# Transposing the attention probabilities with DMA engines in 16-bit halves, in one stage of an eight-layer kernel on Trainium2

## What is computed

```python
q = (hidden_states @ Wq).reshape(B, Sq, H, D)          # H = 16 heads, D = 128
k = (encoder_hidden_states @ Wk).reshape(B, Skv, H, D)
v = (encoder_hidden_states @ Wv).reshape(B, Skv, H, D)
q = rmsnorm(q, gq); k = rmsnorm(k, gk)
scores = jnp.einsum('bqhd,bkhd->bhqk', q, k) * scale
attn = jax.nn.softmax(scores, axis=-1)
out = jnp.einsum('bhqk,bkhd->bqhd', attn, v)
return out.reshape(B, Sq, H * D) @ Wo
...
x = x + jnp.tanh(g_xattn[1]) * _L1_xattn_ref(_layernorm(x, axis=-1), ctx_1024, ...)
```

## Time and profile before

| | |
|---|---|
| median of 3 runs | 1055.78 us (1053.52 to 1056.75) |
| the profiled execution | 1059.89 us |
| its span, first to last instruction | 1058.6 us |
| PE busy | 936.7 us (88%) |
| DVE busy | 725.1 us (68%) |
| ACT busy | 520.7 us (49%) |
| POOL busy | 302.5 us (29%) |
| first attention's loop | about 247 to 554 us of the span |
| PE busy, 285 to 325 us | 40.00 of 40 us, granted clock 1.00 |
| DVE busy, 285 to 325 us | 27.72 of 40 us |
| PE busy, 480 to 520 us | 39.67 of 40 us, granted clock 1.00 |
| DVE busy, 480 to 520 us | 29.76 of 40 us |
| POOL busy, 285 to 325 us | 7.43 of 40 us |

### The profile page before, as it was taken

How to read it: one execution, slowest core, us unless ns; L and a number is a source line. 1 busy time by engine, 2 the same in 40 slices (tenths; PEclk the granted TensorE clock), 3 DMA queues, 4 the chain that set the end, 5 groups by cost and what they waited for, 6 DMA issues and landing times.

```text
span 1058.6 us, 14861 instructions
## 1 busy us (share of the span) xinstructions
PE 936.7 (88%) x4790; PEld 669.3 (63%) x4790; DVE 725.1 (68%) x1877; ACT 520.7 (49%) x1346; POOL 302.5 (29%) x284
## 2 busy tenths in 40 slices
PE   7878789999999999999999989877589988979667
PEld 3323334567999998888977767754355655545455
DVE  5899894245777677678676445576978965576764
ACT  4665672135666666566653434354346552123331
POOL 3767692121111112155101324234232200010210
PEclk8878899999999999999999999999899999989789
DMA  9500001001111164113103446312100003211201
GB/s 363 228 0 0 1 0 50 1 30 45 35 41 46 45 236 153 31 62 94 46 1 119 147 133 191 128 65 60 51 1 1 2 1 141 78 46 31 87 1 41
DMA packets 28500, 75.00 MB, mean 71 GB/s; under 512 B 4092, under 2 KB 5382, under 8 KB 27656
## 3 DMA queue, kind: packets, MB, share of 16 engines
q1 hardware_dynamic: 24344, 63.81, 17.6%
q0 software_dynamic: 3072, 8.39, 2.5%
q10 hardware_dynamic: 1008, 1.86, 0.6%
HBM read 52.03 MB, written 22.02 MB: 70 GB/s over the span
## 4 chain that ended last, share of the span: by engine, by line
PE 62%; DVE 15%; ACT 3%; issue 3%; DMA 1%; SPq 1%; POOL 1%; another core or an unknown queue 0%; DVEq 0%; POOLq 0%; ACTq 0%
PE psum L2195 5%; PE psum L1071 5%; PE psum L1796 5%; PE psum L1277 4%; PE psum L1288 4%; PE psum L927 4%; PE psum L1257 4%; PE psum L1268 2%; PE psum L938 2%; PE psum L1810 2%; PE psum L1095 2%; PE psum L2214 2%; PE psum L2816 2%; PE psum L2458 2%; DVE arena L2492 2%
## 5 line engine op out<-in xcount | busy, mean ns | idle before, releaser
L1167 POOL TENSOR_TENSOR arena<-arena,mhalf 128x8 f32<-128x8 f32 x32 | 53.4, 1670 | 232.6 <-DVE arena L1144 232.6
L1389 DVE SCALAR_TENSOR_TENSOR X<-psum,arena,X 128x256 f32<-128x256 f32 x128 | 56.0, 479 | 64.9 <-PE psum L1288 64.9
L455 POOL TENSOR_TENSOR arena<-arena 128x512 f32<-128x512 f32 x64 | 82.2, 1307 | 8.6 <-PE psum L545 5.1
L855 DVE TENSOR_TENSOR_SCAN arena<-psum,arena 128x512 f32<-128x512 f32 x64 | 74.8, 1210 | 7.9 <-ACT psum L711 6.8
L1331 ACT ACTIVATE arena<-psum,arena 128x256 f32<-128x256 f32 x128 | 59.9, 477 | 35.9 <-DVE arena L1368 33.5
L1796 PE MATMUL psum<-arena 128*128 x248 | 66.6, 391 | 10.6 <-DVE arena L1891 8.8
L2477 ACT ACTIVATE arena<-psum,arena 128x240 f32<-128x240 f32 x128 | 57.4, 463 | 32.3 <-DVE arena L2491 16.4
L545 PE MATMUL psum<-arena,ident 128*128 128x512 f32 x128 | 69.4, 669 | 0.1
L1288 PE MATMUL psum<-arena 128*128 128x256 f32 x256 | 65.9, 380 | 1.2 <-DVE X L1389 1.1
L1257 PE MATMUL psum<-arena 128*128 128x256 f32 x256 | 65.8, 380 | 0.0
L1277 PE MATMUL psum<-arena 128*128 128x256 f32 x256 | 65.8, 380 | 0.0
(11 more groups left out here) (367 smaller groups left out, 2255.7 us busy)
## 6 DMA issues: line engine op xcount, KB each, us to landing
arena<-in_w SPq DMA_DIRECT2D x32, 384.0 KB, 3.1
tokens<-arena SPq DMA_DIRECT2D x2, 4096.0 KB, 22.8
arena<-tokens SPq DMA_DIRECT2D x32, 256.0 KB
results<-arena SPq DMA_DIRECT2D x32, 256.0 KB
arena<-in_moe SPq DMA_DIRECT2D x17, 384.0 KB, 3.1
arena<-in_moe SPq DMA_DIRECT2D x4, 1536.0 KB, 12.8
arena<-in_w SPq DMA_DIRECT2D x2, 1024.0 KB, 6.1
arena<-in_gu SPq DMA_DIRECT2D x1, 1280.0 KB, 7.2
```

Source lines behind the costliest of these rows:

```text
L455: nc.gpsimd.tensor_tensor(m.HC[:, v, :], m.Hs[:, v, :], m.Cs[:, s % 2, :], ALU.mult).then_inc(*tick("HC", s, c))
L855: nc.vector.tensor_tensor_scan(m.Hs[:, 2 * (s % 2) + c, :], bank[m.bank_dA[c]], input_of(m, s, c), 0.0, ALU.mult, ALU.add).then_inc(*tick( ...
```

## The change

For units 2 to 61 the four transposes on PE and the copy on ACT go. Their probabilities are stored by `exponentials` in another order of the same size. POOL's `halves(u)` splits the 32-bit words into two planes of 16-bit words (128 x 1024 words in one copy), SP issues one DMA transpose of both planes, and POOL's `joined(u)` puts the turned planes together in `PT`. The attended products and the results move two iterations later (`attend(u - 3)`, `result(u - 4)`), the rings of sums and inverses grow from 4 to 6. SP's weight loads of pass 5 on go to ACT's queue, at the end of the iteration of each second unit; the experts' weights become sixteen transfers of 384 KB on ACT's queue at units 32 to 58. POOL's root of a pass moves from the end of one iteration to the end of the next.

```diff
+    BY_DMA = range(2, 62)
...
+    def cut(self, u):
+        return ("a1_H" if u in self.BY_DMA else "a1_T", u)
+    def turned_over(self, u):
+        return ("a1_J" if u in self.BY_DMA else "a1_PT", u)
...
+def planes(v):
+    return v.bitcast(U16).rearrange("p (n h) -> p h n", h=2)
...
+def a1_turned_sp(k, m, units):
+    for u in units:
+        k.sp.wait_ge(*k.s.at("a1_H", u))
+        if u - 2 in m.BY_DMA:
+            k.sp.wait_ge(*k.s.at("a1_J", u - 2))
+        k.nc.sync.dma_start_transpose(m.turned[u % 2].rearrange("p h (g i) -> p (h g) i", i=P),
+                                      m.halves[u % 2].rearrange("p h n -> p (h n)")).then_inc(*k.s.landed(f"a1_D{u % 2}", u))
...
@@ def attention1_pe @@
     def attend(u):
-        pe.wait_ge(*at("a1_PT", u))
+        pe.wait_ge(*at(*m.turned_over(u)))
...
-        transposed(u)
+        if u not in m.BY_DMA:
+            transposed(u)
...
-        if u >= 1:
-            attend(u - 1)
+        if u >= 3:
+            attend(u - 3)
...
-        if u >= 2:
-            result(u - 2)
+        if u >= 4:
+            result(u - 4)
...
+    attend(m.UNITS - 3)
+    result(m.UNITS - 4)
+    attend(m.UNITS - 2)
+    result(m.UNITS - 3)
     attend(m.UNITS - 1)
...
@@ def attention1_act @@
         if u >= 2:
-            act.wait_ge(*at("a1_T", u - 2))
-        if u >= 4:
-            act.wait_ge(*at("a1_ri", u - 4))
+            act.wait_ge(*at(*m.cut(u - 2)))
+        if u >= 6:
+            act.wait_ge(*at("a1_ri", u - 6))
...
+        if u not in m.BY_DMA:
+            turned(u)
+        if not first and N + 5 < m.PASSES:
+            a1_weights(k, m, N + 5, act, nc.scalar)
+        given(u)
...
@@ def attention1_pool @@
+    def halves(u):
+        pool.wait_ge(*at("a1_E", u))
+        if u - 2 in m.BY_DMA:
+            pool.wait_ge(*at(f"a1_D{u % 2}", u - 2))
+        nc.gpsimd.tensor_copy(m.halves[u % 2], planes(m.Pr[:, u % 2].rearrange("p c j k -> p (c j k)"))).then_inc(
+            *k.s.tick("a1_H", u))
+    def joined(u):
+        pool.wait_ge(*at(f"a1_D{u % 2}", u))
+        pool.wait_ge(*at("a1_A", u - 2))
+        nc.gpsimd.tensor_copy(planes(m.PT[:, u % 2].rearrange("p c i -> p (c i)")),
+                              m.turned[u % 2]).then_inc(*k.s.tick("a1_J", u))
     for u in range(m.UNITS):
         N, first = u // 2, u % 2 == 0
-        if not first and N + 3 < m.PASSES:
-            a1_root_pool(k, m, N + 3)
+        if u in m.BY_DMA:
+            halves(u)
+        if u - 1 in m.BY_DMA:
+            joined(u - 1)
+        if first and 1 <= N < m.PASSES - 2:
+            a1_root_pool(k, m, N + 2)
         step(beside[u // 32])
...
+def weights_act(k, m1, a2, u):
+    experts = [*range(32, 56, 2), 55, 56, 57, 58]
+    if u in experts:
+        sorted_weights_act(k, m1, experts.index(u))
+    if u == 39:
+        a2_weights_act(k, a2)
```

More of the change, by code:

```diff
@@ L1031, in __init__ @@
         self.Kr = k.place(HT, self.NH, HD)
+        k.at = 23856
+        self.halves = [k.place(2, 2 * S, dt=U16)]
+        self.turned = [k.place(2, 2 * S, dt=U16) for _ in range(2)]
+        assert k.at <= FIRST
+        k.at = LAST - 512
+        self.halves.append(k.place(2, 2 * S, dt=U16))
+    def cut(self, u):
+        return ("a1_H" if u in self.BY_DMA else "a1_T", u)
+    def turned_over(self, u):
+        return ("a1_J" if u in self.BY_DMA else "a1_PT", u)
     @staticmethod
@@ L1042, in mamba_left, with a1_weights, attention1_sp @@
     eng.wait_ge(*k.s.at("HC", 31, 1))
[L1045 to L1055, removed]
+def planes(v):
+    return v.bitcast(U16).rearrange("p (n h) -> p h n", h=2)
+def a1_weights(k, m, N, eng, queue):
+    if N >= 2:
+        eng.wait_ge(*k.s.at("a1_P", N - 2, 1))
+        if N - 2 < m.NH:
+            eng.wait_ge(*k.s.at("a1_M", N - 2))
+    queue.dma_start(m.W[:, N % 2, :], k.io["w1"][N % m.NH]).then_inc(*k.s.landed(f"a1_w{N % 2}", N))
+def attention1_sp(k, m):
+    mamba_left(k, k.sp)
+    a1_weights(k, m, 0, k.sp, k.nc.sync)
+    k.nc.sync.dma_start(m.ctok, k.io["ctok"]).then_inc(*k.s.landed("ctok_in"))
+    for N in range(1, 5):
+        a1_weights(k, m, N, k.sp, k.nc.sync)
+def a1_turned_sp(k, m, units):
[5 more added lines that the diff above has]
+                                      m.halves[u % 2].rearrange("p h n -> p (h n)")).then_inc(*k.s.landed(f"a1_D{u % 2}", u))
 def a1_project_pe(k, m, N, q):
@@ L1326, in exponentials, with turned @@
         if u >= 2:
[L1327 to L1329 removed]
+            act.wait_ge(*at(*m.cut(u - 2)))
+        if u >= 6:
+            act.wait_ge(*at("a1_ri", u - 6))
         for j in range(2):
[L1331 to L1332 removed]
+            e = nc.scalar.activation(m.Pr[:, w, :, j, :], bank[w][:, j * S:(j + 1) * S].rearrange("p (c k) -> p c k", c=2),
+                                     ACT.Exp,
+                                     bias=m.nb[:, w, j:j + 1], scale=m.SCALE, accum_out=m.rs[:, u % 6, j:j + 1])
         e.then_inc(*tick("a1_E", u))
+    def turned(u):
+        act.wait_ge(*at("a1_T", u))
+        if u >= 2:
+            act.wait_ge(*at("a1_A", u - 2))
+        nc.scalar.copy(m.PT[:, u % 2, :, :],
+                       bank[2 + u % 2].rearrange("p (t d) -> p t d", t=2)).then_inc(*tick("a1_PT", u))
     exponentials(0)
@@ L1403, in attention1_dve @@
         inverse(u)
[L1404 to L1407, removed]
+        if u >= 3:
+            attended(u - 3)
+        if u >= 4:
+            result(u - 4)
         if first and N + 2 < m.PASSES:
@@ L1412, in attention1_dve @@
         step(beside[u // 32])
+    attended(m.UNITS - 3)
+    result(m.UNITS - 4)
+    attended(m.UNITS - 2)
+    result(m.UNITS - 3)
     attended(m.UNITS - 1)
```

43 lines of the change are left out of this document (22 added, 21 removed).

## The result

The changed kernel takes 1087.08 us (median of 4 runs, 1082.02 to 1089.06), the kernel before, run beside it, 1056.26 us (4 runs, 1053.52 to 1058.48): ratio 1.0286, 95% interval 1.0243 to 1.0328. It is slower, by about 30 us where the prediction said 8.7, and outside the forecast's own range of 1057 to 1072 us. The profiled execution has a span of 1085.8 us against 1058.6, so 27.2 us are to be found in the traces.

A forecast was written before the change was run, and what follows sets the result against it. PE's groups back to back were taken as the bound, with little slack on ACT and DVE behind. -7.2 + 4.0 + 4.2 + 7.7 = +8.7 us on 1055.78 gave 1064.5 us; range 1046 to 1095, the forecast's own 1057 to 1072.

The forecast's parts named there:

- a slow landing of the transfers: Rival, chance 0.20: DMA transposes land in 5.5 to 8 us, costing +20 to +85 us over 28 passes, so 1075 to 1140.
- Passes with queries only: First attention, 12 passes projecting queries only: PE loses its transposes, saving 0.6 us a pass, -7.2 us in all.
- The ACT issue: New weight issue on ACT's queue, costing 0.45 us out of the 0.82 us ACT is free in queries-only passes.
- Passes with keys too: First attention, 16 passes projecting keys too: about -0.1 us, plus 0.35 for DVE waiting on POOL: +0.25 each, +4.0 in all.
- Unit 34: POOL waits for DVE's `result(31)`, copies of units 34 to 36 stand behind, the power comes late: +4.2 us, once.
- Units 42 to 49: Two scatters an iteration stand on POOL beside the copies: together +7.7 us.
- POOL's queue: Units 42 to 49: POOL's pass 11.1 us against 10.4, +2.8 us; copies queued before the power at the start, +3.9.
- the exclusion with DVE: DVE operations with two SBUF inputs wait for POOL: 0.35 us a keys-too pass, about 1 us at units 42 to 49.
- The transfer: DMA transpose, from `halves` to landing: taken as 4 us, bounds 2.1 and 12.8; up to about 5 mostly covered.
- the estimate of 10.5 us: DMA transpose as eight 128x128 blocks in series: 10.5 us, a loss of some 5 us in each of 28 passes.
- The copies: POOL's copies of 128 x 1024 16-bit words: 1.05 us each, range 0.9 to 1.3.
- Moved work: Two units' attended products and results, 3.4 us, leave the start of the attention and join its end: 0.

The follow-up runs named there:

- experiment 2: The changed kernel with POOL's two copies cut to 8 words per plane from unit 6 on: 1060.32 us, ratio 0.9996 to the kernel before.
- experiment 8: The changed kernel with DVE's small operations reading PSUM and POOL's root ahead of the copies from unit 24 on: 1072.8 us, ratio 1.0121.
- experiment 1: The changed kernel with row maxima and sums of squares written to a free PSUM bank: 1079.0 us, ratio 1.0171.
- experiment 6: The changed kernel with the first attention's weights issued on SP's queue again, behind the transposes of odd units: 1086.48 us, ratio 1.0248.
- experiment 9: The changed kernel with the sorted stage's head begun at unit 36, not 34, on every engine: 1082.99 us, ratio 1.0260.
- experiment 4: The kernel before with POOL's two copies per unit added, results unused, exponentials waiting for the first copy, root behind the copies: 1081.86 us, ratio 1.0196.

## Why the prediction was right, and where its sizes were off

The sign and the places were right: slower, from units 34 and 42 to 49, with a small gain in the queries-only passes. The sum of +8.7 us was a third of what came. That 1087 us still lies in the full range of 1046 to 1095 is luck: the room above 1072 was given to a slow landing of the transfers, which did not happen (3.1 us). In the two places that make the loss, the way in which it arises was only half foreseen.

**Passes with queries only**: -0.6 us each predicted, -0.26 measured. Without the copies it is -0.49 (9.15 to 8.66, experiments 2 and 8), so the loop over PE and ACT was read nearly right, though by the prediction's own numbers ACT had 0.82 - 0.45 = 0.37 us to give and not 0.6; the other 0.23 us goes with the small operations beside `joined` (experiment 1; L1414 in the rows above), which no step of the prediction had. The ACT issue that was charged against this is free in the changed kernel (experiment 6).

**Passes with keys too**: +0.25 predicted, +0.25 measured (9.84 to 10.09), but for partly other reasons. Without copies the pass saves 0.44 us (9.40, experiment 2) and not 0.1. The copies then cost 0.69 and not 0.35: 0.40 through one-input operations (experiment 1), the rest through the root's place behind them (experiment 8). Two errors cancelled.

**Unit 34**: +4.2 predicted, +5.7 measured. The wait is there, and the copies of units 34 to 36 pile up behind it, before the root:

```profile
416.15 1.01 POOL L242 TENSOR_TENSOR rstd<-rstd,mhalf 128x4 f32<-128x4 f32 x1 [5.86 <-DVE rstd L235]
...
417.23 3.94 DVE L249 TENSOR_SCALAR xn<-X,mv,rstd 128x256 f32<-128x256 f32 x4
...
417.55 1.10 POOL L1476 COPY arena<-arena 128x1024 uint16<-128x1024 uint16 x1
418.60 1.39 POOL L1483 COPY arena<-arena 128x1024 uint16<-128x1024 uint16 x1
419.90 1.12 POOL L1476 COPY arena<-arena 128x1024 uint16<-128x1024 uint16 x1
...
423.09 1.63 POOL L1200 TENSOR_TENSOR arena<-arena,mhalf 128x8 f32<-128x8 f32 x1
...
424.04 1.92 PE L261 MATMUL psum<-ident,xn 128*128 128x128 f32 x8 [4.08 <-ACT arena L1149]
```

and in the kernel before:

```profile
416.76 1.38 DVE L248 TENSOR_SCALAR xn<-X,mv,rstd 128x256 f32<-128x256 f32 x4
```

But the path is another one than predicted. The normalisation's wait for the root, 1.61 us, is not on the chain that ended last: the next turn (L1128 at 431.88) comes five microseconds after that normalisation has ended. What is on the chain is L249, four one-input operations of the head that last 3.94 us beside the three copies and 1.38 before, then ACT, and then PE, idle for 4.08 us and afterwards at a lower clock. L249 is 2.6 us longer than before, L261 and the scores behind it 1.7; the rest of the 5.7 was not split. With the head two units later (experiment 9) POOL did not wait for result 31, and the same L249 took 1.37 us.

**Units 42 to 49: the term that was mis-sized.** +7.7 us predicted, +21.7 measured in the six late passes. The prediction counted POOL's queue (11.1 us a pass) and gave the exclusion with DVE "about 1", "a guess from the 0.35 above". POOL's queue was read rightly: from 468.60 us on the chain of waits stays on POOL for 11.5 us, and DVE waits 4.10 us for the root at its end (+3.9 predicted). But this happens once. After it the chain goes over DVE, ACT and PE and back, not over `joined` and not over the root, though POOL is busy 45.6 of the 58.3 us of the last four passes. Pieces of it (start, length, what); those before 468.60 stand ahead of the first scatter:

```profile
440.45 1.26 DVE arena L1713
...
445.93 2.05 PE psum L1107 x8
447.97 1.71 PE psum L1310 x4
...
459.55 1.13 PE psum L1107 x8
460.68 0.87 PE psum L1310 x4
...
478.45 1.62 POOL arena L1200
...
483.15 2.71 DVE arena L1414
...
487.63 2.05 PE psum L1107 x8
...
496.99 2.83 DVE arena L2480
...
511.80 2.60 DVE arena L1414
```

Two things stretch it. DVE operations are held beside copies: L1414 twice (2.70 and 2.59 us for 0.17), L2480 (2.81 for 0.18), L1713 (1.32 for 0.19), L1744 (1.37 for 0.42) and L1191 (1.62 for 1.22) are together some 10 us longer on the chain. And the prediction has no term for the clock. PE's granted clock was 1.00 in all six passes before and is 0.78, 1.00, 1.00, 0.69, 0.88 and 0.87 after; in the low passes PE is idle for 3.60, 4.87, 4.07 and 2.73 us before L1107, and groups behind that run at the lower level, 1.2 and not 2.4 GHz: eight matmuls of L1107 take 2.05 us at 445.93 and 1.13 at 459.55. Such groups are 8.1 us longer on the chain than at full clock. As an estimate from these rows, 10 us of held operations, 8 of clock and the one wait of 4.1 for the root come to 22 us, where 21.7 were measured. A held operation can thus be paid twice: for its own length, and for the slower PE behind the wait that it makes. The pass from 441.3 us shows both without a single scatter, 15.53 us against 11.30. By experiments 4 and 2, 11.8 of the 21.7 us come with the copies alone, 5.6 with the new order on POOL without the copies' length, and 4.3 only with both.

**The transfer**: taken as 4 us, it is 3.1, and not a rival any more; the estimate of 10.5 us, eight blocks in series, did not come either. **The copies**: 1.05 us taken for both; `halves` is 1.06 and `joined`, which writes with a stride, 1.40 in the mean, 1.33 where undisturbed. That is 0.3 to 0.4 us a unit more on POOL. **Moved work**: 0 taken; the first two passes are 1.9 us shorter, the last four 1.6 us longer and the stretch behind them 0.7, but the two traces differ by 3.2 us before the attention starts, so this was not settled.

## What to carry to other kernels

Before work goes to an engine with room on it, look not only at its busy share but at what it shuts out: here a change with 148 us of copies on an engine 41% busy made the kernel 30 us slower, and without their length the loss was gone. Two fifths of it went away already when the inputs of two small operations of another engine, 0.17 us each, moved to PSUM. Small operations that pass a value on (a scaled maximum, a mean) sit on the path whatever their size; if they must run beside long GpSimd work, give them a PSUM operand, which here cut a mean of 446 ns to 159. Add the clock to the price of a wait: where TensorE stood for 2.7 to 4.9 us before its projection, the groups behind it ran at the lower level, and in the six late passes this cost about 8 us. And work taken from the busiest engine is worth only the slack of the loops around it: 26.4 us of TensorE time gave 10.4 us in the 18 plain passes even without the copies' length, the long passes took 7.8 back, and over the whole kernel no gain was measurable (ratio 0.9996).

## What the hardware showed that was not expected

- A tensor_scalar of 128x2 between SBUF tiles, 170 ns by itself, lasted 2.70 us beside two GpSimd copies one behind the other: it did not get in between the two (483.15, and 495.78 in experiment 4). The same with its input in PSUM: 159 ns mean over 56. Four of 128x256 (L249) lasted 3.94 us beside three copies and 1.38 without.
- A DMA transpose of 128x1024 16-bit words from SBUF to SBUF took 1.23 us on SP's queue to issue and 3.1 us to land. The weight loads issued beside 60 of them landed in 3.0 us in the median and 6.6 at most (3.1 and 8.0 before).
- A GpSimd copy of 1024 16-bit words per partition took 1.04 us when it read with a stride of two words, 1.33 us when it wrote with one.
